# First input in two parts on two queues, its first chunk rounded by VectorE; two sequences' results summed by ScalarE and GpSimd, stores moved

## What is computed

```python
ada = (timestep_embed @ ada_w + ada_b)[:, None, :]
shift1, scale1, gate1, shift2, scale2, gate2 = jnp.split(ada, 6, axis=-1)
x1 = _ln(x) * (1.0 + scale1) + shift1
qkv = (x1 @ qkv_w + qkv_b).reshape(Bc, Tc, 3, H, DH)
...                                   # attention, MLP; second block: attention
topv, topi = jax.lax.top_k(probs, 2)  # 2 of 8 experts for each token
eo = jnp.einsum('eti,edi->etd', jax.nn.silu(eg) * eu, wd)
moe_out = jnp.einsum('te,etd->td', combine, eo)
return x + (hidden + moe_out)
```

## Time and profile before

| | |
|---|---|
| runs (3) | median 1172.72 us, 1172.37 to 1172.8 |
| profiled execution | 1174.76 us, its span from first to last instruction 1172.9 us |
| mean granted TensorE clock | 0.992 of full speed |
| TensorE busy | 1141.4 us, 97% |
| VectorE, ScalarE, GpSimd busy | 725.7, 645.5, 506.7 us (62, 55, 43%) |
| chain that ended last | TensorE 89%, VectorE 4%, ScalarE, GpSimd and issuing 2% each, DMA 1% |

### The profile page before, as it was taken

One profiled execution on the slowest core, in us unless ns is written; L12 is line 12 of the kernel. 1 busy time (PEld: TensorE's weight loads), 2 busy tenths in 40 slices (PEclk: granted clock), 3 DMA queues, 4 the chain that ended last, 5 costly groups with the idle time before them and its releaser, 6 DMA issues.

```text
span 1172.9 us, 22331 instructions
## 1 busy us (share of the span) xinstructions
PE 1141.4 (97%) x7602; PEld 1018.7 (87%) x7637; DVE 725.7 (62%) x1587; ACT 645.5 (55%) x1840; POOL 506.7 (43%) x566
## 2 busy tenths in 40 slices
PE   8999999999999999999999999999999999998995
PEld 7989999999999999998997788888888888877994
DVE  3666554334543454347777877777777787766556
ACT  4545543444444443455565766766766666674552
POOL 4111131113111311311336775675677588674573
PEclk9999999999999999999999999999999999999998
DMA  9200000000000002014002008930000100023747
GB/s 345 77 1 1 19 2 18 1 1 1 1 19 1 1 1 91 1 46 171 19 18 73 1 1 227 293 93 1 10 20 10 48 18 19 20 69 91 205 111 244
DMA packets 47265, 70.07 MB, mean 60 GB/s; under 512 B 4279, under 2 KB 39355, under 8 KB 46171
## 3 DMA queue, kind: packets, MB, share of 16 engines
q1 hardware_dynamic: 43475, 59.69, 16.8%
q0 software_dynamic: 3408, 8.43, 2.0%
q10 hardware_dynamic: 272, 0.52, 0.1%
HBM read 40.24 MB, written 29.30 MB: 59 GB/s over the span
## 4 chain that ended last, share of the span: by engine, by line
PE 89%; DVE 4%; issue 2%; ACT 2%; POOL 2%; DMA 1%; SPq 0%; POOLq 0%; DVEq 0%; ACTq 0%
PE bank L1878 15%; PE bank L1915 11%; PE bank L2068 10%; PE bank L1946 8%; PE bank L2122 7%; PE bank L1888 5%; PE bank L2213 5%; PE bank L1906 5%; PE bank L2148 4%; PE bank L2008 3%; PE bank L2256 3%; PE bank L2283 3%; PE bank L1896 2%; PE bank L2188 2%; PE bank L2178 2%
## 5 line engine op out<-in xcount | busy, mean ns | idle before, releaser
L592 POOL TENSOR_TENSOR p<-p,rinv 128x512 f32<-128x512 f32 x64 | 66.6, 1040 | 403.5 <-DVE rinv L1424 403.5
L946 ACT ACTIVATE p<-bank,nb,rq 128x128 f32<-128x128 f32 x256 | 113.8, 454 | 89.2 <-DVE nb L1647 89.2
L813 ACT ACTIVATE p<-bank,nmax 128x128 f32<-128x128 f32 x256 | 90.5, 366 | 115.6 <-DVE nmax L1412 115.4
L667 POOL TENSOR_TENSOR qr<-qr,rb 128x512 f32<-128x512 f32 x64 | 82.5, 1289 | 72.1 <-DVE rb L1601 70.6
L1420 DVE COPY pt<-bank 128x512 f32<-128x512 f32 x64 | 44.2, 691 | 106.0 <-PE bank L1896 105.4
L1878 PE MATMUL bank<-cur_hi,wqk_hi 128*128 128x512 f32 x256 | 107.8, 421 | 0.6 <-DVE cur_lo L1361 0.6
L1878 PE MATMUL bank<-cur_lo,wqk_hi 128*128 128x512 f32 x256 | 101.1, 395 | 0.0
L1878 PE MATMUL bank<-cur_hi,wqk_lo 128*128 128x512 f32 x256 | 100.9, 394 | 0.0
L822 ACT ACTIVATE o_hi<-bank,bqkv 128x512 fp32r<-128x512 f32 x64 | 44.2, 690 | 95.9 <-PE bank L1906 95.5
L1428 DVE SCALAR_TENSOR_TENSOR o_lo<-bank,bqkv,o_hi 128x512 fp32r<-128x512 f32 x64 | 48.0, 750 | 49.6 <-ACT o_hi L822 49.6
L1915 PE MATMUL bank<-wo_hi,o_hi 128*128 128x256 f32 x256 | 77.7, 303 | 0.3 <-DVE o_lo L1428 0.2
(11 more groups left out here) (274 smaller groups left out, 3652.4 us busy)
## 6 DMA issues: line engine op xcount, KB each, us to landing
token_scratch<-empty SPq DMA_DIRECT2D x1, 17415.0 KB, 64.8
xs<-token_scratch SPq DMA_DIRECT2D x39, 129.0 KB
wqk_raw<-in_wqk SPq DMA_DIRECT2D x8, 512.0 KB, 9.8
gate<-gates_scratch SPq DMA_DIRECT2D x8, 512.0 KB, 3.8
got_t<-expert_scratch SPq DMA_DIRECT2D x16, 256.0 KB, 4.8
w_raw<-in_w SPq DMA_DIRECT2D x2, 1408.0 KB, 6.0
xres<-in_x SPq DMA_DIRECT2D x4, 512.0 KB, 8.9
wv_raw<-in_wv SPq DMA_DIRECT2D x8, 256.0 KB, 10.0
```

What stands on the lines that cost most here:

```text
L592: nc.gpsimd.tensor_tensor(p1[:, h % 2], p1[:, h % 2], rinv[:, h % 2].unsqueeze(2).broadcast_to([P, GB, T]), ALU.mult).then_inc(a_pn, 1)
L667: nc.gpsimd.tensor_tensor(qr[:, s.u % 2], qr[:, s.u % 2], rb[:], ALU.add).then_inc(g_qr, 1)
L813: last = nc.scalar.activation(p1[:, h % 2, b], bank[3][:, b * T:(b + 1) * T], ACT.Exp, bias=nmax[:, h % 2, b:b + 1], accum_out=rsum[:, h % ...
L946: last = nc.scalar.activation(p2[:, (s.u - 3) % 2, j], bank[3][:, j * T:(j + 1) * T], ACT.Exp, scale=rq[:, (s.u - 3) % 4, j:j + 1], bias=n ...
```

## The change

1. x of group 0 is issued as sequences 0 and 1 on SyncE's queue and 2 and 3 on ScalarE's queue, ahead of `ada_w` there. VectorE takes the statistics of the first two after the first part and of the others after the second.
2. `d_first` is split: `cond_t` (`d_cond`), `ada_bt` (`d_first`), `bqkv` (`d_bqkv`), and `bqkv` is issued behind the first pair's weights. TensorE waits for `cond_t` and `ada_w` alone; the scaling of `bqkv` on ScalarE moves behind the rounding of `wqk`.
3. VectorE rounds chunk 0 into `cur_hi` itself, right after it has written it; ScalarE rounds chunk 1 only. `idle_turns` goes from 23 to 21.
4. The results of sequences 0 and 1 are no longer made by VectorE: ScalarE scales the two expert outputs in place (`weigh`, at the end of steps 36 and 37), GpSimd adds them to `xres` (`pooled_add`, in steps 36, 37, 38, one each, and the fourth behind the last step). VectorE begins with sequence 2 in step 37.
5. Stores: 2 to 5, 0, 6 to 10 ahead of the last four loads, then 11, 1, 12 to 15.

```diff
@@ block.sync
-            load_x(0)
-            sp.dma_start(cond_t[:], ins["cond_t"]).then_inc(d_first, 16)
+            sp.dma_start(xres[:, 0:2, :], ins["x"][0:2].rearrange("b t d -> t b d")).then_inc(d_x[0], 16)
+            sp.dma_start(cond_t[:], ins["cond_t"]).then_inc(d_cond, 16)
             sp.dma_start(ada_bt[:], ins["ada_bt"]).then_inc(d_first, 16)
-            sp.dma_start(bqkv[:], ins["bqkv"]).then_inc(d_first, 16)
             load_pair(0)
+            sp.dma_start(bqkv[:], ins["bqkv"]).then_inc(d_bqkv, 16)
             load_pair(1)
...
-                sp.wait_ge(m_y, 2 * b + 2)
+                if b < POOLED:
+                    sp.wait_ge(m_p, 2 * b + 2)
+                else:
+                    sp.wait_ge(m_y, 2 * (b - POOLED) + 2)
                 sp.dma_start(out[b], xres[:, b]).then_inc(d_out, 16)
...
             for b in range(BA):
                 load_result(b)
-            for b in range(BA - 3):
+            for b in range(POOLED, 6):
+                store_result(b)
+            store_result(0)
+            for b in range(6, 9):
+                store_result(b)
+            for b in range(9, BA - 1):
                 store_result(b)
             for b in range(BA, B):
                 load_result(b)
-            for b in range(BA - 3, B):
+            store_result(BA - 1)
+            store_result(1)
+            for b in range(BA, B):
                 store_result(b)
@@ block.gpsimd
+            def pooled_add(b, k):
+
+                xb = xres[:, b]
+                pool.wait_ge(m_w, 2 * b + k + 1)
+                pool.wait_ge(r_in, 1)
+                if k == 1:
+                    pool.wait_ge(m_p, 2 * b + 1)
+                nc.gpsimd.tensor_tensor(xb, xb, got_t[:, b, k], ALU.add).then_inc(m_p, 1)
...
                     add_input((i - 20) // 3)
+                if FETCHED - 1 <= i < FETCHED + 2:
+                    pooled_add((i - FETCHED + 1) // 2, (i - FETCHED + 1) % 2)
+            pooled_add(1, 1)
@@ block.scalar
                 if c == 0:
+                    act.wait_ge(d_bqkv, 16)
+                    nc.scalar.activation(bqkv[:, 0], bqkv[:, 0], ACT.Copy, scale=SCALE).then_inc(bq_s, 1)
                     act.wait_ge(ada_s, 4)
                     act.wait_ge(n_tp, KD)
...
-                    last.then_inc(n_ev, 1)
-                    act.wait_ge(n_ev, KD)
-                    for k in range(KD):
-                        nc.scalar.activation(cur_hi[:, k], act_t[:, k, 0:GT], ACT.Copy).then_inc(c_hi, 1)
+                    last.then_inc(c_first[1], 1)
+                    act.wait_ge(c_first[1], 1)
+                    nc.scalar.activation(cur_hi[:, 1], act_t[:, 1, 0:GT], ACT.Copy).then_inc(c_hi, KD)
...
+            nc.scalar.dma_start(xres[:, 2:4, :], ins["x"][2:4].rearrange("b t d -> t b d")).then_inc(d_half, 16)
             nc.scalar.dma_start(ada_w[:, :, 0:2 * D], ins["ada_w"][:, :, 0:2 * D]).then_inc(d_ada1, 16)
-            act.wait_ge(d_first, 48)
-            nc.scalar.activation(bqkv[:, 0], bqkv[:, 0], ACT.Copy, scale=SCALE).then_inc(bq_s, 1)
             split_pair(0)
...
+            def weigh(b):
+
+                act.wait_ge(s_v, S_WEIGHT)
+                act.wait_ge(got_at[b][0], got_at[b][1] + 16)
+                for k in range(2):
+                    nc.scalar.activation(got_t[:, b, k], got_t[:, b, k], ACT.Copy,
+                                         scale=weight[:, k, b:b + 1]).then_inc(m_w, 1)
...
                 expert(i)
+                if FETCHED - 1 <= i < FETCHED - 1 + POOLED:
+                    weigh(i - FETCHED + 1)
@@ block.vector
             dve.wait_ge(d_x[0], 16)
-            norm_stats(0)
+            for b in range(2):
+                nc.vector.bn_stats(bn[:, b], xres[:, b])
+            dve.wait_ge(d_half, 16)
+            for b in range(2, GB):
+                last = nc.vector.bn_stats(bn[:, b], xres[:, b])
+            last.then_inc(n_bn, 1)
...
-            norm_ada(0, 0, 0, 0, bank[0])
+            dve.wait_ge(n_tp, 1)
+            for b in range(GB):
+                last = nc.vector.tensor_scalar(act_t[:, 0, b * T:(b + 1) * T], bank[0][:, b * T:(b + 1) * T],
+                                               ada_t[:, 1, 0, b:b + 1], ada_t[:, 0, 0, b:b + 1], ALU.mult, ALU.add)
+            last.then_inc(c_first[0], 1)
+            dve.wait_ge(c_first[0], 1)
+            nc.vector.tensor_copy(cur_hi[:, 0], act_t[:, 0, 0:GT]).then_inc(n_ev, KD)
+            dve.wait_ge(n_ev, KD)
+            for k in range(KD):
+                if k == 1:
+                    dve.wait_ge(c_hi, KD)
+                nc.vector.tensor_tensor(cur_lo[:, k], act_t[:, k, 0:GT], cur_hi[:, k].bitcast(F32),
+                                        ALU.subtract).then_inc(c_lo, 1)
+            dve.wait_ge(d_bqkv, 16)
...
                 if i >= FETCHED:
-                    result(2 * (i - FETCHED))
-                    result(2 * (i - FETCHED) + 1)
-            for b in range(2 * (NT + 3 - FETCHED), B):
+                    result(POOLED + 2 * (i - FETCHED))
+                    result(POOLED + 2 * (i - FETCHED) + 1)
+            for b in range(POOLED + 2 * (NT + 3 - FETCHED), B):
                 result(b)
@@ block.tensor
-            pe.wait_ge(d_first, 48)
+            pe.wait_ge(d_cond, 16)
             pe.wait_ge(d_ada1, 16)
...
-            idle_turns(23)
+            idle_turns(21)
```

More of the change, by code:

```diff
@@ L256, in program @@
         d_first, d_small = sem("d_first"), sem("d_small")
+        d_half, d_cond, d_bqkv = sem("d_half"), sem("d_cond"), sem("d_bqkv")
         d_ada1, d_ada2, d_bg = sem("d_ada1"), sem("d_ada2"), sem("d_bg")
@@ L271, in program @@
         got_at = [(d_w1, 16), (d_w2, 16), (d_wq, 16), (d_wkv, 16), (d_oproj, 16), (d_ada1, 16), (d_ada2, 16), (d_rope, 32),
-                  (d_first, 48), (d_gate, 16 * 2 * NG), (d_router, 32), (d_wd, 16)] + [(d, PAIR) for d in d_ring[4:8]]
+                  (d_first, 16), (d_gate, 16 * 2 * NG), (d_router, 32), (d_wd, 16)] + [(d, PAIR) for d in d_ring[4:8]]
         d_out = sem("d_out")
@@ L290, in program @@
         c_hi, c_lo = sem("c_hi"), sem("c_lo")
+        c_first = [sem(f"c_first{k}") for k in range(KD)]
         a_qp, a_kp, a_vp, a_sp, a_tp, a_pvp, a_op = (
@@ L319, in program @@
         r_in, m_y = sem("r_in"), sem("m_y")
+        m_w, m_p = sem("m_w"), sem("m_p")
+        POOLED = 2
         RV = 11
@@ L376, in attention2 @@
                     expert(u - DRAIN[TILES])
+        FETCHED = A_DONE + 6
         W3_STEP = 5
@@ L1403, in _ @@
             dve.wait_ge(ada_p, 1)
-            dve.wait_ge(d_first, 48)
+            dve.wait_ge(d_first, 16)
             ada_vectors(((0, 0), (1, 1)))
             dve.wait_ge(ada_s, 4)
-            norm_ada(0, 0, 0, 0, bank[0])
+            dve.wait_ge(n_tp, 1)
[12 more added lines that the diff above has]
+            dve.wait_ge(d_bqkv, 16)
             def row_max(n, h):
@@ L1436, in attention1 @@
                     past = background_norm(g, h - 1, first)
-                    if h == 0:
+                    if h == 0 and not first:
                         cur_rest(g, g)
@@ L1782, in result @@
                                                op0=ALU.mult, op1=ALU.add).then_inc(m_y, 1)
-                dve.wait_ge(m_y, 2 * b + 1)
+                dve.wait_ge(m_y, 2 * (b - POOLED) + 1)
                 nc.vector.scalar_tensor_tensor(out=xb, in0=got_t[:, b, 1], scalar=weight[:, 1, b:b + 1], in1=xb,
@@ L1822, in _ @@
             attention2(step)
-            FETCHED = A_DONE + 6
             for i in range(FIRST, NT + 3):
```

## The result

The changed kernel took 1176.44 us in the median of ten runs (1175.01 to 1179.02), the kernel before 1173.03 in ten runs beside it (1171.57 to 1175.23): ratio 1.0029, 95% interval 1.0020 to 1.0039. It is slower by 3.4 us, more than the 0.2% that the prediction called measurable, and above the end of its range, 1174.6. The profiled execution took 1178.76 us, its span 1176.9, 4.0 more than that of before. It is one of the three slowest of the ten, all with a mean granted clock of 0.991; the other seven took at most 1176.84 us, at 0.992 to 0.995. So what the profile shows of the clock need not hold for them.

The account below looks back on a forecast made before the run. TensorE, busy 97% of the span, was taken to bound the kernel, so only head and tail could move time. Head -1.2, adds +1.95, stores -0.4 gave +0.35: 1173.1 us, range 1170.9 to 1174.6.

Parts of the forecast that it names:

- x at 4.0: Head: with its halves on two queues, x lands at about 4.0 us instead of 4.75, 0.77 us sooner.
- The rival built on it, at 1173.6: Head: splitting x brings nothing, halves land at 4.7, only 0.65 saved; +0.9 in all, 1173.6 us; chance 0.14.
- ada_w at 6.9: Head: ada_w starts at about 4.0, shares with the pair weights, takes 2.9 us and lands at 6.9; transposes gain 0.55.
- The bounds of the head: Head: the projection starts 1.2 us earlier (0.55 + 0.65), with bounds of 0.5 and 1.6 saved.
- Chunk 0 on VectorE: Head: transposes to projection take 3.52 to 3.7 us instead of 4.24, a gain of 0.55 to 0.7.
- the case that the copy meets wqk_lo: Head: VectorE's copy cannot start before GpSimd's wqk_lo ends at up to 11.63; the head saves about 0.8.
- bqkv covered: Head: bqkv lands at about 8.5, needed by ScalarE at 10.1; costs nothing, 1 us if late.
- weigh: Tail, ScalarE: scaled copies delay x_hi(37) by 0.56 us, of which 0.17 reaches VectorE's first result.
- The adds exclude VectorE: Tail: GpSimd's adds hold VectorE for 0.67, 0.45 and 0.68; last loads 1.95 us later, bounds 0.15 and 2.6.
- The first rival (adds in gaps): Tail: GpSimd's adds cost VectorE next to nothing, loads move 0.15; -1.45 in all, 1171.3 us; chance 0.25.
- the third (GpSimd starved): Tail: back-to-back VectorE results keep GpSimd's add waiting, loads 4.8 us later; +3.2 in all, 1175.9 us; chance 0.05.
- Stores: Tail: ten stores ahead of the last loads covered by 1.3 us; one less beside them saves 0.4, bounds 0 and 1.0.

Follow-up runs that it names:

- h6: Head of the change alone, but both halves of x on SyncE's queue and ada_w first on ScalarE's; ratio 1.0031 to the kernel before.
- h1: Head of the change alone (x in two parts, d_first split, bqkv later, chunk 0 rounded by VectorE), tail as before; ratio 1.0004 to the kernel before.
- h4: h1 with ada_w's first part in two halves, one on each queue, SyncE's ahead of the first pair's weights; ratio 0.9987 to the kernel before.
- f1: The whole change, but with ada_w's first part in two halves, one on each queue; ratio 1.0010 to the kernel before.
- f2: The whole changed kernel run once more, unchanged, on another chip; ratio 1.0026 to the kernel before.
- t3: Tail of the change with the four GpSimd adds, stores 0 and 1 and both weigh calls behind everything else, head as before; ratio 0.9999 to the kernel before.
- t2: Tail of the change with the four GpSimd adds and stores 0 and 1 behind everything else, weigh in place, head as before; ratio 1.0001 to the kernel before.
- t1: Tail of the change alone (weigh on ScalarE, adds on GpSimd, stores moved), head as before; ratio 1.0013 to the kernel before.
- t4: The kernel before with results 9 and 10 also stored ahead of the last loads, eleven stores there; ratio 1.0003 to the kernel before.
- g1: h1 run again, unchanged, on another chip; ratio 1.0008 to the kernel before.
- g2: t1 run again, unchanged, on another chip; ratio 1.0014 to the kernel before.
- h2: h1 with 38 idle turns instead of 28 ahead of ada_columns; ratio 1.0001 to the kernel before.

## Why the prediction was wrong, and where it was right

- **x at 4.0: right for its first half** (4.09; the other profiles with x on two queues have 3.95 to 4.20). The second landed at 4.25 to 4.46, and the statistics of the first two sequences filled the time between. The Trainium skill ("DMA: Bandwidth & Descriptors", Issuing engines are not separate DMA queues) has a second issuer save only the time of issuing. For the landing of one piece the trace disagrees in part: whole on one queue x landed at 4.42 to 4.77, not much behind the second half on two, but in halves on one, with ada_w beside it from the start, at 3.54 and 5.91 (h6). It agrees that the queues share: ada_w, pushed back, lost more than x gained. The rival built on it, at 1173.6, failed with its mechanism; its rounding, 0.65, was right.
- **ada_w at 6.9: the step that failed.** "It shares with the pair weights: 512 KB at 177 GB/s are 2.9" took half of a rate read at 3 to 4 us, and held it until the end of the transfer. Behind half of x ada_columns started at 7.21 to 8.73 in seven profiles; in that of after ada_w landed at 8.41, so 512 KB in 4.4 us, some 120 GB/s. Half a rate was about right up to 6 us (195 GB/s), but not by sharing: the pair weights hardly ran, and all transfers together moved 222 GB/s at 4 to 6 us instead of 348 in before. From 6 us on, beside the weights, ada_w had 9% of the engines' time and not half: its last 0.08 MB, 0.5 us at the forecast's rate, took 2.4. h1 has the same: 0.40 MB against 0.06 from 4 to 6, then 0.10 against 0.76. The bounds of the head, 0.5 to 1.6 saved, let no loss in, though the term had no row: nothing in the trace of before showed ada_w alone beside the weights. h4 and f1 show that its place in the queues is the cause. Why ada_w gets so little beside the weights, and why the weights hardly run before 6 us, stays open.
- **The clock was not in the sum.** At equal clock the head costs 0.1 to 0.4, the tail 1.9: 2.0 to 2.3, and the changed kernel's ten runs lie 2.5 and 2.2 above the lines of before in the first two groups (if they ran on that chip, which is not known). The rest of the 3.4, about 1, is put down to the clock by argument: f2's mean clock was 0.0015 under before's, worth about 1 at 0.5 to 0.7 us for each 0.001; that of the ten runs was only 0.0005 to 0.0011 under before's in these groups, worth 0.3 to 0.6; the clocks of before's ten runs beside them aren't known. That TensorE with less to do at 7 to 9 us may lose its clock was no rival, and should have been one: a moved transfer made a new wait on the critical engine.
- **Chunk 0 on VectorE: right.** From the transposes to the projection 3.66 in h1 (14.04 less 10.38), forecast 3.52 to 3.7; the copy 0.43, forecast 0.5. The Trainium skill ("SBUF — State Buffer", Who interferes with whom) was weighed as a loss of the head's gain for the case that the copy meets wqk_lo. It did in h4: 1.00 instead of 0.43, held until wqk_lo ended at 11.84. The trace agrees; in the changed kernel the late ada_w had taken the copy past it.
- **bqkv covered: right in effect.** It landed at 10.5 instead of 8.5 and was still done before chunk 1 needed ScalarE.
- **weigh: mis-sized.** Two scaled copies take 0.90, pitch 0.40, not 0.28 as taken; x_hi(37) starts 1.08 behind its expert_out, in t3 0.29, so 0.79 later instead of 0.56. VectorE's first result starts 0.60 later (0.13 behind the expert_out of 1154.67, in t3 0.47 ahead of its), not 0.17. Of that weigh has 0.38, as t2 shows; the rest goes with the goal of tile 37, which took 0.42 instead of 0.21 beside the first add.
- **The adds exclude VectorE: right.** Forecast 0.67 + 0.45 + 0.68 = 1.80. Measured in the lengths: results 0.30 and 0.35 up to x_lo(38), then goal 0.13 and results 0.39 and 0.47: 1.64, with the goal of tile 37 1.85. With weigh's 0.38 that is 2.23, and h(38) is 2.29 late; forecast 1.95. The single instructions were lengthened by less than forecast, to 0.78 to 0.95 instead of 1.1 to 1.2, and more of them were. The wait before gate_up(38), 0.86, is the 0.8 of the prediction. The first rival (adds in gaps) and the third (GpSimd starved) are out: each deliver came in its turn.
- **Stores: the cover right, the gain not shown.** Load 14 took 4.43, forecast 4.6; but in t1, with the same tail, it took 4.91, near the 4.99 of before, and from the expert_out named to the end were 22.75 us (1175.0 less 1152.25), 2.19 more than before and not 1.67. So what the moved stores give lies between 0.1 and 0.6 in two profiles, and 4.43 may be chance. The cover held: the loads went out at 1167.46, the ten stores were issued by 1166.11 (1156.12 plus 9.99). t4, with eleven and without the adds, shows a delay of 0.73 where that cover is gone.
- **Sum.** In the place of -1.2 for the head stand +0.1 to +0.4, in that of 1.95 - 0.4 for the tail stands +1.9, and the clock, which had no term, adds 0.3 to 1: 2.3 to 3.3, measured 3.4 (2.3 to 4.6 by the interval). The largest part of the miss, 1.3 to 1.6, is the head, by way of ada_w; the tail is 0.35 of it.

## What to carry to other kernels

Splitting a transfer over a second queue puts what was first in that queue second: name the one that is pushed back, and who waits for it, before counting what comes early. A landing that no row of the trace shows deserves bounds on the losing side too, more so if the busiest engine waits for it. And one profile can show a fall of the clock that other executions of the kernel don't have: count it over several before pricing it. Adds of another engine in the shadow of VectorE's last instructions are not free when both read two operands from SBUF: they were worth 1.7 us here merely by being moved behind the last delivery.

## What the runs showed of the hardware

- TensorE's granted clock fell to one half for some 3 to 7 us at a time, once 10, ahead of the end of the span: at 9 to 16 us in six of 18 profiled executions, at 1060 to 1110 in all but one (h1). The same kernel had it in one profile and not in another (h1 and g1, t1 and g2). The head of the change had it more often, by the count above; the fall began with TensorE idle in h6 and with TensorE busy for over 2 us in h2. What sets it off is not settled.
- A scaling from SBUF to SBUF with one input (xn, f32) was held by GpSimd's wqk_lo like the instructions with two: 3.47 against 1.38.
- On the first chip an execution's mean clock went with most of the spread of the spans of the kernel before: 0.5 and 0.7 us for each 0.001, 72% and 80% of the variance. In the group of f1 it was 0.3 and 7%.
- Beside 0.70 MB that another queue moved, 0.08 MB of ada_w took 2.4 us in the profile of after; most of it had moved at 195 GB/s just before.
